# A fixed tile for each expert in a mixture-of-experts layer, and TensorE's expert program unrolled

## The reference

```python
probs = sigmoid(x @ router_w.T + expert_bias)     # 160 experts
top_w, top_idx = top_k(probs, 8)
top_w = top_w / (sum(top_w) + 1e-9) * 2.5
h1 = silu(einsum('th,eih->eti', x, w_gate))       # inner width 64
routed = einsum('eti,ehi->th', h1 * combine.T, w_down)
shared = silu(x @ w_gate_shared.T) @ w_down_shared.T
return routed + shared
```

## Time and profile before

| what | us |
|---|---|
| median of three runs | 2896.11 (2887.38 to 2908.32) |
| the profiled execution | 2902.76 |
| its span | 2900.9 |
| expert groups of run 0, both halves | 447 to 930 |
| expert groups of run 1, both halves | 1319 to 1800 |

### The profile page before, as it was taken

One profiled execution on the slowest core, in us unless ns is written; L12 is line 12 of the kernel. 1 busy time (PEld: TensorE's weight loads), 2 busy tenths in 40 slices (PEclk: granted clock), 3 DMA queues, 4 the chain that ended last, 5 costly groups with the idle time before them and its releaser, 6 DMA issues.

```text
span 2900.9 us, 44112 instructions
## 1 busy us (share of the span) xinstructions
PE 1753.3 (60%) x13716; PEld 1146.8 (40%) x13716; DVE 1334.2 (46%) x3558; ACT 970.8 (33%) x1719; POOL 1057.4 (36%) x1177
## 2 busy tenths in 40 slices
PE   3765506776666454556776676422325488888975
PEld 2544404555444242244554454100124234455443
DVE  3648811222334677473222333543215466666644
ACT  3651102232223321312232222356761123444342
POOL 2001777724651774757714651771000200000000
PEclk9985557778878655557788787655555568998985
DMA  8941118999997111117999997120000000000001
GB/s 234 382 181 29 51 53 275 325 304 292 321 289 241 52 52 54 52 55 244 327 308 294 310 301 241 51 54 8 4 2 0 0 1 1 1 1 2 1 1 29
DMA packets 332506, 393.39 MB, mean 136 GB/s; under 512 B 57952, under 2 KB 222512, under 8 KB 332208
## 3 DMA queue, kind: packets, MB, share of 16 engines
q1 hardware_dynamic: 215616, 171.43, 19.0%
q10 hardware_dynamic: 83984, 153.13, 15.4%
q0 software_dynamic: 32768, 67.17, 7.7%
HBM read 242.13 MB, written 164.63 MB: 140 GB/s over the span
## 4 chain that ended last, share of the span: by engine, by line
PE 36%; DVE 15%; DMA 13%; ACT 11%; issue 10%; SPq 9%; POOL 6%; DVEq 0%; ACTq 0%; POOLq 0%
DMA arena<-expert_blocks 12%; SPq L1819 6%; ACT arena L955 5%; PE psum L1918 4%; PE psum L1909 4%; POOL slot_rows L1725 4%; PE psum L448 3%; SPq L1815 3%; PE psum L1347 2%; PE psum L1900 2%; PE psum L1328 2%; PE psum L432 2%; PE psum L993 1%; PE psum L427 1%; ACT arena L1210 1%
## 5 line engine op out<-in xcount | busy, mean ns | idle before, releaser
L1736 POOL DMA_INDIRECT arena<-slot_results,SLOTS x512 | 490.7, 958 | 503.1 <-DMA slot_results<-arena 285.8
L1725 POOL DMA_INDIRECT slot_rows<-arena,SLOTS x512 | 493.4, 964 | 309.4 <-issue 308.8
L1699 DVE COPY arena<-psum 128x512 f32<-128x512 f32 x288 | 198.6, 690 | 742.3 <-PE psum L1918 719.4
L1909 PE MATMUL psum<-arena 128*64 128x128 f32 x2304 | 236.5, 336 | 278.4 <-DMA arena<-expert_blocks 271.0
L1779 ACT ACTIVATE arena<-psum 128x512 f32<-128x512 f32 x288 | 171.9, 597 | 476.4 <-PE psum L1900 467.6
L1909 PEld LDWEIGHTS psum<-arena 128*64 128x64 f32 x2304 | 154.5, 165 | 349.0 <-issue 291.5
L169 POOL TENSOR_SCALAR rstd<-mv 128x4 f32<-128x4 f32 x32 | 6.2, 193 | 772.3 <-DVE mv L577 771.8
L1900 PE MATMUL psum<-ident,arena 128*128 128x128 f32 x1152 | 231.6, 335 | 84.9 <-DMA arena<-slot_rows 84.3
L1918 PE MATMUL psum<-arena 64*128 64x128 f32 x2304 | 253.3, 350 | 0.0
L1786 ACT ACTIVATE arena<-psum 128x256 f32<-128x256 f32 x288 | 110.4, 383 | 338.5 <-PE psum L1909 335.3
L1918 PEld LDWEIGHTS psum<-arena 64*128 64x128 f32 x2304 | 189.6, 230 | 64.4 <-issue 64.2
(11 more groups left out here) (234 smaller groups left out, 3064.5 us busy)
## 6 DMA issues: line engine op xcount, KB each, us to landing
arena<-expert_blocks SPq DMA_DIRECT2D x1152, 96.0 KB
arena<-slot_rows ACTq DMA_DIRECT2D x288, 256.0 KB
slot_results<-arena ACTq DMA_DIRECT2D x288, 256.0 KB
slot_rows<-zeros SPq DMA_DIRECT2D x2, 18432.0 KB, 84.2
slot_rows<-arena,SLOTS POOLq DMA_INDIRECT x512, 2.2
arena<-slot_results,SLOTS POOLq DMA_INDIRECT x512
expert_blocks<-in_expert_w SPq DMA_DIRECT2D x1, 7680.0 KB, 26.0
expert_blocks<-in_expert_w SPq DMA_DIRECT2D x1, 5120.0 KB, 52.7
```

Source lines behind the costliest of these rows:

```text
L1699: dve.tensor_copy(YSB[:, p].rearrange("p (c h) d -> p h c d", h=2), psum[:, first:first + 2, 0:256].rearrange("p h (c d) -> p h c d", c=2) ...
L1725: pool.indirect_dma_start(out=slot_rows[h], out_offset=bass.IndirectOffsetOnAxis(ap=SLOTS[:, t, k:k + 1], axis=0), in_=XNH[:, t], in_offse ...
L1736: pool.indirect_dma_start(out=GATHERED[:, t % TPI, k], out_offset=None, in_=slot_results[h], in_offset=bass.IndirectOffsetOnAxis(ap=SLOTS[ ...
L1909: mm = pe.matmul(psum[lo:lo + INTER, 2 + 5 * (p % 2), o:o + P], EWB[:, p, q, 0:INTER], XSBT[:, p, P * q:P * q + P], start=True, stop=True, ...
```

## The change

The 288 slot tiles of a half are laid out otherwise. The first 160 belong one to each expert ("own" tiles, 40 groups); the first 128 pairs of an expert go there. The other 128 tiles (32 groups, "more") take what overflows, by count as before. `GROUP_ORDER` mixes the groups of the two kinds nearly in turn.

For the own groups the experts are known beforehand, so their weights come from a second copy, `own_blocks`, in one transfer of 256 KB with 2 KB for each partition (two experts' gate weights lie beside each other, their down weights one above the other), at a fixed address. The "more" groups keep the registers and the four transfers. `own_blocks` is made by four more DMAs at the start, between the copies to `expert_blocks` and the zero fill.

A slot number now has two cases: `rows_of_slots` compares it with the end of the expert's own tile and adds `DELTA` where it is beyond. Adding no longer keeps the eight numbers of a token in expert order, so a running sum over the four tiles is taken, masked, its eight largest found and neighbours subtracted. `place` loses its max. Six of the sixteen calls of `rows_of_slots` (the last three of half 1 in each run) move in among the copies of half 0's first ten groups. TensorE's and SyncE's expert loops become straight code. The rest of the kernel is as before.

```diff
@@
+        OWN_GROUPS = NE // GROUP
+        MORE_GROUPS = GROUPS - OWN_GROUPS
+        GROUP_ORDER = sorted(range(GROUPS), key=lambda n: (n + 0.5) / OWN_GROUPS if n < OWN_GROUPS else (n - OWN_GROUPS + 0.5) / MORE_GROUPS)
...
+        OWN_W = GROUP * (INTER + D // 2)
...
+        own_blocks = nc.dram_tensor("own_blocks", (P, OWN_GROUPS * OWN_W), F32).ap()
...
+        def own_tiles(dve):
+
+            dve.tensor_tensor_scan(OWN_END, ones_row[:], ones_row[:], 0.0, ALU.mult, ALU.add).then_inc(o_own, 1)
+            dve.wait_ge(o_own, 1)
+            dve.tensor_scalar(OWN_END, OWN_END, float(P), None, ALU.mult).then_inc(o_own, 1)
+            dve.wait_ge(o_own, 2)
+            dve.tensor_scalar(OWN, OWN_END, -float(P), None, ALU.add).then_inc(o_own, 1)
...
-            dve.tensor_scalar(COUNT, COUNT, P - 1, None, ALU.add).then_inc(link.sem, link.one())
+            dve.tensor_scalar(COUNT, COUNT, -1, None, ALU.add).then_inc(link.sem, link.one())
...
+            dve.tensor_scalar(NTILES, NTILES, 0.0, None, ALU.max).then_inc(link.sem, link.one())
+            dve.wait_ge(link.sem, link.so_far())
...
         def place(dve, run, t):
 
-            j = t % TPI
             dve.wait_ge(s_a.sem, s_a.at(run, t))
-            if j == 0:
-                dve.wait_ge(s_idx.sem, s_idx.before(run, t // TPI))
-            dve.scalar_tensor_tensor(SLOTM[:, j], psum[:, 7, 0:NE], 1.0, MASK[:, t, :], ALU.add, ALU.mult).then_inc(s_slotm.sem, 1)
-            dve.wait_ge(s_slotm.sem, s_slotm.at(run, t))
+            dve.scalar_tensor_tensor(SLOTM[:, t % HTILES], psum[:, 7, 0:NE], 1.0, MASK[:, t, :], ALU.add, ALU.mult).then_inc(s_slotm.sem, 1)
+
+        def rows_of_slots(dve, run, i):
+
+            link = Order(s_slot, run, i)
+            placed = SLOTM[:, TPI * (i % HSTEPS):TPI * (i % HSTEPS) + TPI]
+            every = lambda row: row.unsqueeze(1).broadcast_to([P, TPI, NE])
+            dve.wait_ge(s_slotm.sem, s_slotm.at(run, TPI * i + TPI - 1))
+            dve.tensor_tensor(OVER, placed, every(OWN_END), ALU.is_gt).then_inc(link.sem, link.one())
+            dve.wait_ge(link.sem, link.so_far())
+            dve.tensor_tensor(OVER, OVER, every(DELTA), ALU.mult).then_inc(link.sem, link.one())
+            dve.wait_ge(link.sem, link.so_far())
+            dve.tensor_tensor(OVER, placed, OVER, ALU.add).then_inc(link.sem, link.one())
+            dve.wait_ge(link.sem, link.so_far())
             stand(dve)
-            dve.max(S8[:, j], SLOTM[:, j]).then_inc(s_s8.sem, 1)
-            if j == TPI - 1:
-                rows_of_slots(dve, run, t // TPI)
-
-        def rows_of_slots(dve, run, i):
-
-            dve.wait_ge(s_s8.sem, s_s8.at(run, TPI * i + TPI - 1))
-            dve.tensor_scalar(SLOT[:], S8[:], -1.0, None, ALU.add).then_inc(s_slot.sem, 1)
...
+            dve.tensor_tensor_scan(PLACED.rearrange("p t e -> p (t e)"), ones_row[:, 0:1].broadcast_to([P, TPI * NE]), OVER.rearrange("p t e -> p (t e)"),
+                                   0.0, ALU.mult, ALU.add).then_inc(link.sem, link.one())
+            dve.wait_ge(link.sem, link.so_far())
+            dve.tensor_tensor(PLACED, PLACED, MASK[:, TPI * i:TPI * i + TPI, :], ALU.mult).then_inc(link.sem, link.one())
+            dve.wait_ge(link.sem, link.so_far())
+            stand(dve)
+            for j in range(TPI):
+                last = TOPK * (TPI - 1 - j)
+                dve.max(S8[:, last:last + TOPK], PLACED[:, j]).then_inc(link.sem, link.one())
+            dve.wait_ge(link.sem, link.so_far())
+            dve.scalar_tensor_tensor(SLOT[:].rearrange("p t k -> p (t k)"), S8[:, 0:TPI * TOPK], -1.0, S8[:, 1:TPI * TOPK + 1],
+                                     ALU.add, ALU.subtract).then_inc(link.sem, link.one())
...
+            def own_weights(n, p):
+                sp.dma_start(EWB[:, p, :].rearrange("p q c -> p (q c)")[:, 0:OWN_W], own_blocks[:, OWN_W * n:OWN_W * (n + 1)]).then_inc(c_own[p].sem, 16)
+
+            def more_weights(n, p):
+                stand(sp)
...
             sp.wait_ge(o_expert.sem, o_expert.at(run, h))
-            for p in range(UNROLL):
-                if hr:
-                    sp.wait_ge(c_y.sem, c_y.at(hr - 1, GSTEPS - 1, p + 1))
-                stand(sp)
-                weights_of(0, p)
-            with sp.Fori(0, GSTEPS - 1) as g:
-                for p in range(UNROLL):
-                    sp.wait_ge(c_y.sem, c_y.at(hr, g, p + 1))
-                    stand(sp)
-                    weights_of(g + 1, p)
+            for g in range(GROUPS):
+                n, p = GROUP_ORDER[g], g % UNROLL
+                if hr or g >= UNROLL:
+                    sp.wait_ge(c_y.sem, c_y.at(hr, 0, g - UNROLL + 1))
+                if n < OWN_GROUPS:
+                    own_weights(n, p)
+                else:
+                    more_weights(n - OWN_GROUPS, p)
...
-            with pe.Fori(0, GSTEPS - 1) as g:
-                for p in range(UNROLL):
-                    transposes(g + (p + 2) // UNROLL, (p + 2) % UNROLL)
-                    inner(g + (p + 1) // UNROLL, (p + 1) % UNROLL)
-                    results(g, p)
...
+            for g in range(GROUPS):
+                if g + 2 < GROUPS:
+                    transposes(g + 2)
+                if g + 1 < GROUPS:
+                    inner(g + 1)
+                results(g)
...
+                    if h == 0 and t % TPI == TPI - 1 or t == HTILES + TPI - 1:
+                        rows_of_slots(dve, 0, t // TPI)
             for run in range(HALVES):
                 for g in range(GROUPS):
                     results_out(dve, run, 0, g)
+                    if g % 4 == 1 and g // 4 < HSTEPS - 1:
+                        rows_of_slots(dve, run, HSTEPS + 1 + g // 4)
...
+            for u in range(2):
+                sp.dma_start(own_of[:, :, INTER * u:INTER * (u + 1)], pair_of[u, :, :, 0:INTER]).then_inc(blocked, 16)
+                sp.dma_start(own_of[INTER * u:INTER * (u + 1), :, 2 * INTER:], pair_of[u, 0:INTER, :, INTER:]).then_inc(blocked, 16)
```

More of the change, by code:

```diff
@@ L1543, in program @@
         c_ld = [signal(f"c_ld{p}", 16, GSTEPS) for p in range(UNROLL)]
-        c_ew = [signal(f"c_ew{p}", 16 * GROUP, GSTEPS) for p in range(UNROLL)]
+        OWN_IN = [sum(GROUP_ORDER[g] < OWN_GROUPS for g in range(p, GROUPS, UNROLL)) for p in range(UNROLL)]
+        c_own = [signal(f"c_own{p}", 16, OWN_IN[p]) for p in range(UNROLL)]
+        c_more = [signal(f"c_more{p}", 16 * GROUP, GSTEPS - OWN_IN[p]) for p in range(UNROLL)]
         c_st = [signal(f"c_st{p}", 16, GSTEPS) for p in range(UNROLL)]
@@ L1691, in rows_of_slots @@
             dve.tensor_tensor(SLOTS[:, TPI * i:TPI * i + TPI, :], SLOT[:], IN_TILE[:], ALU.bitwise_or).then_inc(s_idx.sem, 1)
+            link.close()
         def results_out(dve, run, h, g):
@@ L1878, in count @@
             mm.then_inc(e_cnt.sem, 1)
-            pe.wait_ge(o_link.sem, o_link.at(run, h))
-            pe.matmul(psum[:, 7, 0:NE], ident[:], FIRST, start=True, stop=True, skip_group_check=True)
+            pe.wait_ge(o_own, 3)
+            pe.matmul(psum[:, 7, 0:NE], ident[:], OWN, start=True, stop=True, skip_group_check=True)
+            pe.wait_ge(o_col.sem, o_col.at(run, h))
             for q in range(GROUP):
@@ L1894, in experts_tensor, with transposes @@
             hr = HALVES * run + h
-            def transposes(g, p):
-                pe.wait_ge(c_ld[p].sem, c_ld[p].at(hr, g))
-                pe.wait_ge(c_xt.sem, c_xt.at(hr, g, p - 1))
+            def transposes(g):
+                p = g % UNROLL
+                pe.wait_ge(c_ld[p].sem, c_ld[p].at(hr, g // UNROLL))
+                pe.wait_ge(c_xt.sem, c_xt.at(hr, 0, g - 1))
                 for q in range(GROUP):
@@ L1901, in transposes, with gate_of, down_of, inner @@
                 mm.then_inc(c_tr.sem, 1)
-            def inner(g, p):
-                pe.wait_ge(c_ew[p].sem, c_ew[p].at(hr, g))
-                pe.wait_ge(c_xt.sem, c_xt.at(hr, g, p + 1))
-                pe.wait_ge(c_he.sem, c_he.at(hr, g, p - 1))
+            def gate_of(g, q):
+                if GROUP_ORDER[g] < OWN_GROUPS:
+                    at = 2 * D * (q // 2) + INTER * (q % 2)
+                    return EWB[:, g % UNROLL].rearrange("p q c -> p (q c)")[:, at:at + INTER]
+                return EWB[:, g % UNROLL, q, 0:INTER]
+            def down_of(g, q):
+                lo = INTER * (q % 2)
+                if GROUP_ORDER[g] < OWN_GROUPS:
+                    at = 2 * D * (q // 2) + 2 * INTER
+                    return EWB[lo:lo + INTER, g % UNROLL].rearrange("p q c -> p (q c)")[:, at:at + D]
+                return EWB[lo:lo + INTER, g % UNROLL, q, INTER:EW]
+            def inner(g):
+                p = g % UNROLL
+                before = sum((GROUP_ORDER[k] < OWN_GROUPS) for k in range(p, g, UNROLL))
+                if GROUP_ORDER[g] < OWN_GROUPS:
+                    pe.wait_ge(c_own[p].sem, c_own[p].at(hr, before))
+                else:
+                    pe.wait_ge(c_more[p].sem, c_more[p].at(hr, g // UNROLL - before))
```

(19 more changed lines are left out.)

78 lines of the change are left out of this document (42 added, 36 removed).

## The result

The changed kernel takes 2877.03 us (median of 8, 2860.5 to 2887.65), where the kernel before, on the same chip, takes 2893.5: a ratio of 0.9936 [0.9917, 0.9956]. Beside a later run of the kernel before, at 2897.9, it took 2872.19, 0.9913 [0.9888, 0.9938]. It is faster by 0.6 to 0.9%, 17 to 26 us, where 59 were forecast. 2877 lies inside the range of 2780 to 2900, but well off 2837. The two profiled executions lie further apart, 2900.9 and 2872.2 us of span, since the one of the kernel before took 9 us more than its median and the other 3 us less.

What follows compares the result with a forecast made beforehand. The prediction took the DMA engines beside GpSimd's traffic, and SyncE's issue without it, as the bounds. -90 us in the stages and +31 for tails gave -59: 2902.8 to 2844 profiled, median 2837 us (chance 0.5), range 2780 to 2900.

Steps and rivals of the forecast that it cites:

- There the 16 DMA engines are full: Expert groups beside GpSimd's dispatch and gather: DMA engines set the pace, at shares up to 0.97; SyncE's issue elsewhere.
- the gain of 90 us in the stages: Expert stages: 22 us less in half 0 and 23 in half 1, over two runs -90 us.
- Does the ring of four buffers allow this pace?: Expert weight buffers: SyncE's 3.0 us plus a 4.8 us landing allow 2.75 us a group, under 3.08.
- the 2.76 assumed alone: Groups without GpSimd's traffic: 2.76 us each at a DMA share of 0.93, without SyncE's limit.
- the 3.08 beside dispatch: Half 0's groups beside GpSimd's dispatch: 3.08 us each, from 2.57 us of engine time over 0.834.
- The mean group of 2.57 us for 2.85: DMA engine time a group: 2.34 us for own, 2.85 for "more", mean 2.57, where every group took 2.85.
- no limit: SyncE's issue in the expert groups: falls to about 1.6 us a group and no longer sets the pace.
- Tails: VectorE's address tail: 7.3 us, 5.8 more; costs 7.1 in run 0, 20.7 in run 1, 3 between group copies: +31.
- What was put at nothing: Four more copies at the start (about 35 us, covered), TensorE's straight code and its fetching: no cost or gain in the sum.
- The DMA engines fill up: Rival, chance 0.15: with SyncE out of the way the DMA share goes to 1.00 everywhere; 2796 us.
- TensorE becomes the bound: Rival, chance 0.2: at the lower clock a group takes TensorE 3.25 us; 2899 throughout, 2868 half the way.
- the own transfers are slow: Rival, chance 0.15: pieces 80 KB apart make own transfers dear; 2927 us at 1.29 us each, 2979 at 1.56.

Runs made afterwards that it cites:

- run 0: Not a follow-up: the first of two runs inside one kernel execution, each with two halves of expert groups; its expert stage took 483.0 us before, 459.0 changed.
- run 1: Not a follow-up: the second of two runs inside one kernel execution; its expert stage took 481.2 us before, 445.5 changed.
- own groups first: The changed kernel, four weight buffers, with each half's 40 own groups ahead of its 32 "more" groups instead of mixed: 2814.2 us, ratio 0.9713.
- the longer tails: The changed kernel with the three 640-wide operations that make `OVER` in VectorE's address tail done three times over: 2946.1 us, ratio 1.0150.
- contiguous: The changed kernel with eight weight buffers and `own_blocks` laid out so each own group's 256 KB is one run: 2714.2 us, ratio 0.9361.
- the other order: The changed kernel with eight weight buffers and each half's 40 own groups ahead of its 32 "more" groups: 2732.9 us, ratio 0.9424.

## Why the prediction was wrong

The step that failed is the first one, "There the 16 DMA engines are full". From it came a group's price in engine time, and from that the gain of 90 us in the stages; two thirds of it came.

By the traces the stages are 59.7 us shorter (24.0 and 35.7) and the rest is 31.1 longer: 10.6 ahead of run 0's groups, 17.6 between the stages, 2.9 behind them. Together that is 28.6 us of span less, where 59 were forecast. Of the forecast's 31 us for the tails 3 belong inside the stages, so it stood at -87 inside and +28 elsewhere. Inside, 27 of the 87 are missing, and that is the miss. Elsewhere the two stretches that have a term give 28.2, but by luck: 10.6 came for 7.1 and 17.6 for 20.7. No term covers the 2.9 behind the stages; that stretch varies by 4 us from version to version, and the stages of the changed kernel differ by 5 us between its two profiles.

- **"There the 16 DMA engines are full" (failed; the cause).** The share of 0.97 was read as a limit. The kernel before with eight buffers moves its bytes at 353 and 361 GB/s in the same windows, for 321 and 305; own groups first takes 58 us off the changed kernel without a byte less. Nor is a packet's time in the profile a fixed price: queue q10 took 2.98 us/MB, in the kernel before with eight buffers 2.78 (50.4% of 156 us for 28.24 MB), and in the changed kernel with eight 2.71 (53.2% of 161 us for 31.58 MB). So 2.85 and 2.57 us of engine time a group were no prices that add up. The page of the kernel before had the hint: its second slice of 72.5 us, copies and zero fill at the start, moves 382 GB/s. What set the pace beside the dispatch was what the prediction had seen without it, SyncE's own work: 12 us of waits in 157. The change lifts that for 40 of 72 groups, and then the turn of the ring is next.
- **"Does the ring of four buffers allow this pace?" (failed, a mis-sized term).** The right question, with a landing of 4.8 us from one row. The seven landings of the chain above have a mean of 5.97 us; the chain runs through the long ones. With 3.0 + 6.0 = 9.0 for 7.8 the prediction's formula gives w = (9.0 - 0.66 - 3.86) / 2 = 2.24 and (3.86 + 2.24) / 2 = 3.05 us a group, over the 2.76 assumed alone and about the 3.08 beside dispatch; with a landing of 8 us it is 3.55. Measured are 3.19, 3.00, 3.31 and 3.00 in the four windows of run 0.
- **The mean group of 2.57 us for 2.85 (not borne out).** With four buffers the single transfer gives 0.01 us of the forecast 0.28 in the stretch without GpSimd. With eight it gives 0.22, but there SyncE's four issues are a limit that it lifts, so the engine time stays unshown. That the stages got shorter nonetheless comes for the most part from what SyncE is spared: register loads, and perhaps the steps of its loop, which the prediction had booked as "no limit" or not at all.
- **Tails (the operations right, the stretches only in sum).** From 276.81 to 284.06 the tail takes 7.25 us, 7.3 forecast. VectorE's timeline in the changed kernel:

```profile
276.81 0.82 DVE L1703 TENSOR_TENSOR arena<-arena 128x640 f32<-128x640 f32 x1
...
279.49 1.49 DVE L1710 TENSOR_TENSOR_SCAN arena<-ones_row,arena 128x640 f32<-128x640 f32 x1
...
281.99 1.01 DVE L1718 MAX8 S<-arena 128x8 f32<-128x160 f32 x4
...
283.87 0.19 DVE L1729 TENSOR_TENSOR SLOTS<-SLOT,IN_TILE 128x32 int32<-128x32 int32 x1
```

  The stretch between the stages grew from 389.0 to 406.6, 17.6 for 20.7. Run 0's groups begin 10.6 later and not 7.1: the dispatch starts 4.6 later (280.5, 285.1) and itself got 5.8 longer (below). That three tails go among the first groups for next to nothing stands only as a sum with the other terms; the longer tails show how near that was to its edge.
- **What was put at nothing (right but for one thing left out).** TensorE's straight code alone is worth nothing, and q8 moves 108 packets at 0.2% in the changed kernel. The Trainium skill, "Runtime: NRT & Kernel Launch", section "Instruction fetch mechanics", prefers unrolled code; 1.0019 [1.0003, 1.0035] shows no gain by it here. The zero fill landed at 217.3 us, 36.7 later than before (35 forecast), well ahead of the dispatch at 285.1. SyncE's straight code has no term in the prediction: its queue goes from group to group in 0.11 us for the loop's 0.30, in a kernel where SyncE hardly waits.
- **The rivals.** "The DMA engines fill up": a share of 1.00 came only with eight buffers. "TensorE becomes the bound" and "the own transfers are slow" fell by the runs above; no loss at a pitch of 80 KB was found (2711.4 us, contiguous 2714.2; an own transfer 0.84 us), so the Trainium skill's figure for row pitches of large powers of two ("DMA: Bandwidth & Descriptors", section "Latency and other measured facts") does not carry over to it. The case that came, a ring whose turn paces the changed kernel, had been dismissed in one paragraph and had no chance of its own.

The version with eight buffers, 2711.4 us, beats both kernels. What paces it is not settled: a share of 1.01 to 1.03 is no proof, as seen, but contiguous weights left it where it was (2714.2) and the other order made it slower (2732.9). How the 60 us off the stages split between registers, SyncE's straight code, issues and transfer on the chips at 2897 us was not measured.

## What to carry to other kernels

Here a DMA share near 1 said that transfers were under way, and not that the engines could do no more. Compare the GB/s with the best window of the same kernel, and count how long the queue that issues the transfers waits: where it hardly waits, its own instructions are the pace, whatever the share. Before pricing bytes, follow one buffer round its ring (wait, issue, landing, use) with the longest landings, not one. Where the turn divided by the depth is near the pace, try depth first: on a slower chip two more buffers were worth about as much as the whole change (0.030 and 0.029 of the time). Work in the gaps of another engine cost little that could be seen at 7.3 us, and one for one what was added to that.

## What the runs showed of the hardware

**GpSimd's indirect DMAs are slower to issue beside wide VectorE operations.** The changed kernel, GpSimd's and VectorE's timelines from 286 to 292 us:

```profile
286.62 0.96 POOL L1768 DMA_INDIRECT slot_rows<-arena,SLOTS  x1 [0.30 <-issue]
287.89 1.56 POOL L1768 DMA_INDIRECT slot_rows<-arena,SLOTS  x1 [0.31 <-issue]
289.76 2.13 POOL L1768 DMA_INDIRECT slot_rows<-arena,SLOTS  x1 [0.30 <-issue]
```

```profile
287.79 0.82 DVE L1705 TENSOR_TENSOR arena<-arena 128x640 f32<-128x640 f32 x1
288.65 0.82 DVE L1707 TENSOR_TENSOR arena<-arena 128x640 f32<-128x640 f32 x1
289.62 1.49 DVE L1710 TENSOR_TENSOR_SCAN arena<-ones_row,arena 128x640 f32<-128x640 f32 x1
```

An issue of 0.96 us takes up to 2.13 while the tail runs. Of the 128 issues of half 0, none took over 1.3 us before, 7 did in the changed kernel and 19 with the longer tails. That dispatch took 161.6, 167.4 and 172.9 us from its first issue to the start of its last: some 6 us for three tails of 7.3, and 5.5 for 15 us of tail more.

**Chips differ by a quarter for this program.** On two of them the kernel before takes 3584 to 3589 us. From 520 to 600 us, while GpSimd dispatches half 1, the chain of waits of the kernel before with TensorE's code straight stands still for tens of microseconds in which nothing that the profile shows is waited for (two more pieces there, of 17.67 and 11.15 us, are put down to "another core or an unknown queue"):

```profile
552.14 22.01 issue
574.18 34.28 issue
```

Its window of half 1's dispatch (columns of the earlier trace rows) has 80 matrix instructions, four groups, where 47 groups are done on the other chips:

```profile
515.00:662.00 147.00, 13.80 (x80) 9.64 (x78) 2.27 (x8) 4.82 (x8) 111.39 (x117) 0.51 0.20 65
```

Why was not looked into. The change is worth 2.9% there and 0.6 to 0.9% on the others.
